# A conv-plus-experts block on one core: statistics of the first norm moved to ScalarE, sums and waits regrouped, and a new order on every engine

## What is computed

```python
x = x + conv(ln_c(x))              # ln_c: norm over the 128 channels, eps 1e-6
#   q, k, v = projections with Wq, Wkv and biases; 8 heads of 16
#   Q, K = elu(q) + 1, elu(k) + 1
#   out = causal_sum(Q, K, V) / (Q . cumsum_over_heads(K) + 1e-10)
t = x as (image, token, channel)
t = t + ffn(ln_t(t))               # ln_t: norm over the 128 channels, eps 1e-5
#   logits = t @ gate_w + router_gamma; probs = softmax; top 2 of 8 experts
#   out = sum over experts of combine * (gamma_e * (t @ expert_w[e] + expert_b[e]) + beta_e)
```

## Time and profile before

| | |
|---|---|
| median of 3 runs | 684.3 us (683.94 to 686.49) |
| the profiled execution | 687.47 us |
| its span, first to last instruction | 685.7 us |
| busy: TensorE, VectorE | 623.9 us (91%), 626.5 us (91%) |
| busy: GpSimd, ScalarE | 501.6 us (73%), 437.5 us (64%) |
| granted TensorE clock, mean over the span | 0.989 |
| DMA, mean over the span | 45 GB/s |

### The profile page before, as it was taken

One profiled execution on the slowest core, in us unless ns is written; L12 is line 12 of the kernel. 1 busy time (PEld: TensorE's weight loads), 2 busy tenths in 40 slices (PEclk: granted clock), 3 DMA queues, 4 the chain that ended last, 5 costly groups with the idle time before them and its releaser, 6 DMA issues.

```text
span 685.7 us, 37586 instructions
## 1 busy us (share of the span) xinstructions
PE 623.9 (91%) x13936; PEld 506.3 (74%) x14044; DVE 626.5 (91%) x2175; ACT 437.5 (64%) x1549; POOL 501.6 (73%) x745
## 2 busy tenths in 40 slices
PE   4769989999999999999999999999999999998875
PEld 3657777777777777777777777777777777777663
DVE  6778989999999999999999999999999999999774
ACT  1337656666667777666666667776776666667643
POOL 4747767777778888887778877878787787766631
PEclk9989999999999999999999999999999999999997
DMA  5211110111111111111111111111111121111001
GB/s 131 78 34 34 34 48 8 47 49 50 47 46 46 46 46 46 46 46 46 46 46 46 46 46 46 46 46 46 46 46 46 46 62 31 32 34 34 19 19 31
DMA packets 60234, 30.58 MB, mean 45 GB/s; under 512 B 2160, under 2 KB 60176, under 8 KB 60176
## 3 DMA queue, kind: packets, MB, share of 16 engines
q1 hardware_dynamic: 60176, 29.79, 15.5%
HBM read 20.34 MB, written 9.44 MB: 43 GB/s over the span
## 4 chain that ended last, share of the span: by engine, by line
PE 52%; DVE 24%; issue 15%; POOL 5%; DVEq 1%; ACT 1%; POOLq 0%; ACTq 0%
DVE total L824 4%; PE wide_b L1005 4%; PE num L1116 4%; PE wide_a L1212 4%; PE num L1081 3%; PE num L1099 3%; PE wide_a L1213 3%; PE wide_a L1214 3%; DVE bn L649 3%; DVE probs L696 3%; PE wide_a L1062 3%; DVE o L834 2%; PE bank_g L1037 2%; PE bank_g L975 2%; PE bank_g L1022 2%
## 5 line engine op out<-in xcount | busy, mean ns | idle before, releaser
L497 ACT ACTIVATE part<-wide_a,scale 128x128 f32<-128x128 f32 x576 | 156.3, 382 | 2.5 <-PE wide_a L1214 1.0
L373 POOL TENSOR_TENSOR two_sums<-part 128x512 f32<-128x512 f32 x72 | 92.9, 1290 | 32.0 <-ACT part L497 30.4
L1212 PE MATMUL wide_a<-e_high,x_high 128*128 128x512 f32 x216 | 97.8, 453 | 3.1 <-issue 1.1
L460 ACT ACTIVATE q_eo<-bank_g,parity 128x512 f32<-128x512 f32 x72 | 49.7, 690 | 67.5 <-PE bank_g L1037 67.5
L1214 PE MATMUL wide_a<-e_high,x_low 128*128 128x512 f32 x216 | 85.6, 396 | 0.0
L1213 PE MATMUL wide_a<-e_low,x_high 128*128 128x512 f32 x216 | 85.4, 395 | 0.0
L317 POOL TENSOR_TENSOR k_sum<-k_sum,feat 128x64 f32<-128x64 f32 x216 | 72.6, 336 | 16.9
L359 POOL TENSOR_TENSOR pack<-weight,pack 128x64 fp32r<-128x64 f32 x36 | 22.2, 616 | 77.1 <-ACT pack L505 77.1
L824 DVE SCALAR_TENSOR_TENSOR total<-wide_b,scale,total 128x128 f32<-128x128 f32 x216 | 58.8, 342 | 0.0
L824 DVE SCALAR_TENSOR_TENSOR total<-wide_a,scale,total 128x128 f32<-128x128 f32 x216 | 58.8, 342 | 0.0
L1212 PEld LDWEIGHTS wide_a<-e_high,x_high 128*128 128x128 f32 x216 | 41.6, 193 | 21.1 <-issue 17.2
(11 more groups left out here) (175 smaller groups left out, 2003.6 us busy)
## 6 DMA issues: line engine op xcount, KB each, us to landing
x<-in_x SPq DMA_DIRECT2D x36, 256.0 KB, 3.0
x_res<-in_x SPq DMA_DIRECT2D x36, 256.0 KB, 3.6
out<-o SPq DMA_DIRECT2D x36, 256.0 KB, 3.1
e_raw<-in_L_ffn_expert_w SPq DMA_DIRECT2D x1, 512.0 KB
beta_raw<-in_L_ffn_beta_w SPq DMA_DIRECT2D x1, 512.0 KB
w_raw<-in_L_conv_Wkv SPq DMA_DIRECT2D x2, 64.0 KB, 2.4
b_qkv<-in_L_conv_bkv SPq DMA_DIRECT2D x1, 128.0 KB, 5.9
w_raw<-in_L_conv_Wq SPq DMA_DIRECT2D x1, 64.0 KB, 2.6
```

Source lines behind the costliest of these rows:

```text
L373: tt(two_sums[:, g.par, two], part[:, two, 0:2], part[:, two, 2:4], ALU.add).then_inc(S[f"two_sums{p}"], 1)
L460: nc.scalar.activation(q_eo[:, g.par, :, e], bank_g[:].rearrange("p (u t) -> p u t", t=T), copy, scale=parity[:, e:e + 1]).then_inc(S[done ...
L497: last = nc.scalar.activation(part[:, u, e], w_bank[B_BANK[u]][:, 128 * e:128 * e + 128], copy, scale=scale[:, g.par, u, 4 + e:5 + e])
L1212: mm(out, x1_high[:, g.par, u], e_high[:, four], start=True, stop=False)
```

## The change

**First norm.** `statistics` and `variances` leave VectorE, with the `memset`. ScalarE now makes two passes over the four transposed images in `bank_g`: the first copies with scale and accumulates the mean, the second squares with that mean as bias and accumulates the variance. Each pass is four activations with an accumulator; the second waits for the first.

**Denominators.** `denominators_eps` moves from VectorE to ScalarE.

**Unit steps.** `add_parts` and `experts_1_to_4` handle one image instead of two, with a semaphore for each. GpSimd's four sums have 256 columns instead of two of 512. VectorE still has 16 operations a group; both halves of `two_sums` now start a sum, so that `total` has two rows and `output` transposes these.

**Coefficients.** `coef_transposed` writes `bank_o` instead of `bank_g`, and waits for `o_done` of the group before; `coefs` reads it there.

**Waits.** In the loop, the waits of `from_state`, `values` and `key_values` are put ahead of the last row of the work before them (`ahead`), and the three loads of zeros are gone. At the edges they stay.

**Order.** Every `step` is written in another order with other ages, and VectorE's and GpSimd's pipelines have 5 steps instead of 6, SP's 6 instead of 9.

**Set-up.** Five `memset`s (state, `v_pad`, `coef_t`) move from VectorE to GpSimd, and `w_t` is copied ahead of `place`.

The diff, cut to its core:

```diff
+            def means(g):
+                need(act, "squares1_done", g.i)
+                need(act, "xt_done", g.i + 1)
+                for u in range(U):
+                    last = nc.scalar.activation(squares[:, u], bank_g[:, T * u:T * u + T], copy, scale=-ROOT / CH,
+                                                accum_out=mean1[:, u:u + 1])
+                last.then_inc(S["means_done"], 1)
+
+            def variances(g):
+                need(act, "means_done", g.i + 1)
+                need(act, "ve1_done", g.i - 1)
+                for u in range(U):
+                    last = nc.scalar.activation(squares[:, u], bank_g[:, T * u:T * u + T], ACT.Square, scale=ROOT,
+                                                bias=mean1[:, u:u + 1], accum_out=ss1[:, g.par, u:u + 1])
+                last.then_inc(S["squares1_done"], 1)
...
+            def denominators_eps(g):
+                need(act, "rden_done", g.i)
+                need(act, "den_sum", g.i + 1)
+                nc.scalar.activation(den1[:], den[:], copy, bias=1e-10).then_inc(S["den_eps"], 1)
...
-            def add_parts(g, p):
-                need(pool, f"part{2 * p}", g.i + 1)
-                need(pool, f"part{2 * p + 1}", g.i + 1)
+            def add_parts(g, u):
+                need(pool, f"part{u}", g.i + 1)
                 need(pool, "out_done", g.i - 1)
-                two = slice(2 * p, 2 * p + 2)
-                tt(two_sums[:, g.par, two], part[:, two, 0:2], part[:, two, 2:4], ALU.add).then_inc(S[f"two_sums{p}"], 1)
+                tt(two_sums[:, g.par, u], part[:, u, 0:2], part[:, u, 2:4], ALU.add).then_inc(S[f"two_sums{u}"], 1)
...
+                add(0, two_sums[:, g.par, u, 0]).then_inc(done, 1)
+                add(2, two_sums[:, g.par, u, 1]).then_inc(done, 1)
+                dve.wait_ge(done, 2 * g.i + 1)
+                add(1, total[:, g.par, u, 0])
+                dve.wait_ge(done, 2 * g.i + 2)
+                add(3, total[:, g.par, u, 1]).then_inc(S[f"a_sum{u}"], 1)
...
-            def coef_transposed(g):
+            def coef_transposed(g, ahead=None):
                 need(pe, "coef_low", g.i + 1)
-                need(pe, "bn_done", g.i + 6)
+                need(pe, "o_done", g.i)
...
+                if g:
+                    experts(g, 0, 0, (lambda: values_ready(n)) if early else None)
+                g = at(4)
+                if g:
+                    values(g, early)
```

More of the change, by code:

```diff
@@ L514, in coefs @@
                     rows = slice(ROWS * u, ROWS * u + ROWS)
-                    last = nc.scalar.activation(coef_t[rows, g.par, T * u:T * u + T], bank_g[rows, 0:T], copy)
+                    last = nc.scalar.activation(coef_t[rows, g.par, T * u:T * u + T], bank_o[rows, 0:T], copy)
                 last.then_inc(S["ct_evac"], 1)
@@ L643, in expert_weights @@
                              ALU.mult, ALU.subtract))
-            def statistics(g):
-                need(dve, "stats_done", g.i)
-                need(dve, "xt_done", g.i + 1)
-                for u in range(U):
-                    last = nc.vector.bn_stats(bn[:, u], bank_g[:, T * u:T * u + T])
-                last.then_inc(S["bn_done"], 1)
-            def variances(g):
-                need(dve, "bn_done", g.i + 1)
-                need(dve, "ve1_done", g.i - 1)
-                nc.vector.memset(pause[:], 0.0)
-                for u in range(U):
-                    last = nc.vector.bn_aggr(mv1[:, g.par, u], bn[:, u])
-                last.then_inc(S["stats_done"], 1)
             def project(g, u):
@@ L1135, in x1_centred @@
                     need(pe, "lg_done", g.i)
+                    need(pe, "o_done", g.i - 1)
                 for u in range(U):
+                    if u == U - 1 and ahead:
+                        ahead()
                     out = bank_g[:, WIDE * u:WIDE * (u + 1)] if u < IN_G else bank_o[:, 0:WIDE]
@@ L1227, in output @@
                 for u in range(U):
-                    out = bank_o[:, T * u:T * u + T]
-                    mm(out, two_sums[:, g.par, u, 1], ident[:], start=False, stop=False, is_transpose=True,
-                       skip_group_check=True)
-                    last = mm(out, total[:, g.par, u], ident[:], start=False, stop=(u == U - 1), is_transpose=True,
-                              skip_group_check=True)
+                    if u == U - 1 and ahead:
+                        ahead()
+                    for k in range(2):
+                        last = mm(bank_o[:, T * u:T * u + T], total[:, g.par, u, k], ident[:], start=False,
+                                  stop=(u == U - 1 and k == 1), is_transpose=True, skip_group_check=True)
                 last.then_inc(S["out_done"], 1)
@@ L1281, in step @@
                     experts(g, 1, 1)
[L1282 removed]
+                n = at(4)
+                early = bool(n and not n.edge)
+                if g:
+                    experts(g, 0, 0, (lambda: values_ready(n)) if early else None)
                 g = at(4)
                 if g:
[L1285 removed]
+                    values(g, early)
                 g = at(5)
@@ L1295, in step @@
                 g = at(5)
+                n = at(3)
+                early = bool(n and not n.edge)
                 if g:
-                    experts(g, 3, 0)
+                    experts(g, 3, 0, (lambda: key_values_ready(n)) if early else None)
+                g = at(3)
+                if g:
+                    key_values(g, early)
+                g = at(5)
+                if g:
+                    experts(g, 2, 0)
+                g = at(1)
+                if g:
+                    project(g, 2)
+                    project(g, 3)
+                g = at(3)
+                if g:
+                    if first(g):
+                        router()
+                    q_transposed(g)
+                g = at(1)
+                if g:
+                    project(g, 1)
+                    project(g, 0)
             steps(pe, step, 6)
```

429 lines of the change are left out of this document (207 added, 222 removed).

## The result

The changed kernel takes 784.15 us (median of four runs, 782.29 to 799.96), the kernel before 684.74 in the same session. The ratio is 1.144, 95% interval 1.140 to 1.147: slower by a seventh, where 645.7 us and a gain were forecast. The run of 799.96 us was a slow one, over 1.5% above the fastest, and is not in the ratio. The profiled execution has a span of 782.5 us against 685.7.

What follows compares the result with a forecast made beforehand. VectorE was taken as the bound, TensorE half a microsecond behind. A turn of 16.45 instead of 17.43 us gave loop 24.5, turns ahead 5.9, filling and set-up 1.2 + 3, end 4: 38.6 off 684.3, so 645.7 us; range 628 to 664.

Steps and rivals of the forecast that it cites:

- GpSimd has room: GpSimd's four unit sums replace two longer ones: 0.4 us more a turn, absorbed because others rarely wait for it.
- TensorE* does the same matmuls: TensorE's loop: matmuls unchanged, three loads of zeros gone; its turn becomes 16.1 to 16.9 us, 16.5 chosen.
- ScalarE's passes: First norm's statistics on ScalarE: eight accumulating activations, 0.25 us each in the first pass, 0.34 in the second.
- the rival that ended slower: ScalarE's two passes do not overlap accumulator readings, so ScalarE sets the pace at 18.0 us a turn: 696 us; chance 0.07.
- The wait for the unit sum: At VectorE's first expert sum: VectorE waits 0.2 us a turn for ScalarE's and GpSimd's work.
- `coef_transposed` waiting for the output: On TensorE, `coef_transposed` now waits for `o_done`, VectorE's output; costed at nothing.
- The ring through the keys' copy: ScalarE's `pexp` ahead of the keys' copy, which frees `bank_g`: eats the gain, 17.4 us a turn, 680 to 684; chance 0.05.
- The 1.31: VectorE loses `bn_stats`, `memset`, `bn_aggr` and the epsilon: 1.31 us less a turn, from 17.43 to 16.1.
- The wait of `rden` for the epsilon: On VectorE, `rden` waits for the epsilon queued on ScalarE: 0.4 us a turn.
- they cost nothing there: VectorE keeps 16 expert operations in steps of two, so the unit sums add nothing on it.
- TensorE's zeros: Removing the three loads of zeros from TensorE's loop saves 0.4 us a turn, between 0 and about 0.8.
- The set-up: Ahead of the first projection: moved `memset`s let it start at about 11 instead of 14.11, 3 us saved.

Runs made afterwards that it cites:

- e1: The changed kernel with 64 loads of zeros put once into TensorE's set-up: 727.27 us, ratio 1.0625 to the kernel before.
- e4: e1 with GpSimd's queries-times-keys product waiting for VectorE's ranks of the others and the low part of x behind it: 678.52 us, ratio 0.990.
- e12: e4 with GpSimd's long product waiting for VectorE's equal instead of the ranks behind it: 672.2 us, ratio 0.980.
- e9: e4 with VectorE's router chain filled as in the kernel before and ScalarE's router exponential moved behind values and keys: 677.17 us.
- e7: e4 with ScalarE's router exponential moved from ahead of the values and keys to behind them: 677.37 us.
- e5: e4 with the three loads of zeros back in every turn of TensorE's loop, each behind its own waits: 681.48 us.
- e8: e4 with the first norm's statistics on VectorE again and none on ScalarE: 700.89 us, ratio 1.023.
- e2: The kernel before with 195 loads of zeros put once into TensorE's set-up: 789.43 us, ratio 1.151.
- e3: The kernel before with 100 loads of zeros put once into TensorE's set-up: 693.24 us, ratio 1.011.
- e11: The kernel before with 165 loads of zeros put once into TensorE's set-up: 708.17 us, ratio 1.034.

## Why the prediction was wrong, step by step

**The frame.** That GpSimd has room and that SP costs nothing were answers to one question only, who waits for whom by semaphores; the text ahead of the prediction says that the engines meet only there. Both causes of the loss lie outside that: GpSimd held VectorE up without a semaphore (62 rows of e1), and TensorE stood still for its own code. The step that failed first is GpSimd's, "0.4 more a turn, and has room": its price was right (a unit sum takes 745 ns, 0.74 was taken), but nobody asked what its moved operations stand beside.

```profile
L374 POOL TENSOR_TENSOR two_sums<-part 128x256 f32<-128x256 f32 x144 | 105.8, 745 | 54.4 <-ACT part L527 53.5
```

The orders of both engines were there to be read: `x_low` and `qk` had moved to where VectorE runs the router's chain. 1.6 us a group, 49 us (e1 to e4), and 6 more to e12. The second failure is "*TensorE* does the same matmuls". It does, and its loop is even a record shorter; but the set-up and the edge turns ahead of it changed length, and its code came to lie on seven marks: 57 us (after to e1), the lower clock behind the stalls included. No term, no rival and no chance stood for it. The trace of before did show the transfers that end at 176 us and begin again at 600, but the prediction didn't read them.

**What held.** ScalarE's passes, in after, are 0.26 (forecast 0.25) and 0.36 (0.34) apart:

```profile
418.12 0.28 ACT L436 ACTIVATE squares<-bank_g 128x128 f32<-128x128 f32 x1 [0.26 <-PE bank_g L977]
...
418.38 0.27 ACT L436 ACTIVATE squares<-bank_g 128x128 f32<-128x128 f32 x1
...
419.29 0.37 ACT L444 ACTIVATE squares<-bank_g,mean 128x128 f32<-128x128 f32 x1
...
419.65 0.36 ACT L444 ACTIVATE squares<-bank_g,mean 128x128 f32<-128x128 f32 x1
```

So ScalarE doesn't set the pace; the rival that ended slower named the wrong engine and the wrong mechanism. The wait for the unit sum is 0.2 as forecast (the distance at the residual add, 0.79 against 0.62). `coef_transposed` waiting for the output is real and cost nothing, as said (e9). The ring through the keys' copy is real and cost nothing (e7).

**What was mis-sized**, seen once both causes are out of the way (distances of VectorE's starts a group, us, mean of 20 groups of before, e4 and e1):

| rows of VectorE | before | e4 | e1 |
|---|---|---|---|
| statistics, epsilon | 1.31 | 0 | 0 |
| output | 0.81 | 0.60 | 0.60 |
| residual add | 0.62 | 0.79 | 0.77 |
| 16 expert rows | 4.21 | 4.37 | 4.42 |
| key-value masks | 0.40 | 0.54 | 0.54 |
| first two router rows | 0.37 | 0.65 | 0.65 |
| two hot rows | 0.45 | 0.78 | 0.49 |
| logits of the others, equal, ranks | 0.53 | 0.52 | 2.25 |
| hot sum, weight | 0.34 | 0.58 | 0.58 |
| all rows | 17.46 | 17.19 | 18.78 |

The 1.31 and the 0.2 of the output went as forecast. The wait of `rden` for the epsilon, forecast 0.4, is 0.1 in e4; it was in after, where ScalarE was late, 16.5 us in 28. What was left out are the rows that the new order made longer: the expert rows, "they cost nothing there", 0.16; the key-value masks, the router's first two rows, the hot sum and weight together 0.7; and `hot`, held by GpSimd, 0.3. So the turn is 17.19 and, without most of the hold, 16.96 (e12), not 16.45. TensorE's zeros were put at 0.4 and are 0.15 (e5). The set-up was put at 3 us; the first projection comes only 1.0 earlier than in the earlier trace rows, at

```profile
13.10 0.67 PE L1007 MATMUL wide_b<-w_high,x_high 128*128 128x384 f32 x1
```

because TensorE waited 3.78 us for `w_t` and 1.24 for `w_low` ahead of it, and not for the second `x`.

**The sum.** From 784.2: 57 us for the code, 49 and 6 for the contention, leads to 672.2. Of the 26.5 from there to the forecast, the starts of the outputs place 24. In the kernel before the first starts at 79.38 us, the 7th, the 32nd and the last as in the earlier trace rows; in e12 these four start at 78.00, 185.29, 609.18 and 667.72. So the 25 groups of the loop gain 11.8 us and not 24.5, the six ahead of them 3.6 and not 5.9, set-up and filling 1.4 and not 4.2, and the last four groups, which were to gain 4, lose 2.2. The first two go with VectorE's longer turn; what makes the end slower is not shown. The mechanism that the prediction counted on, work from a full engine to one with room, is there and is worth 22 us (e8). It was outweighed by two costs that no row of a wait announces.

## What to carry to other kernels

Before a loop of many matmuls is changed, or anything ahead of it, count its TensorE instructions and see over how many 16 KB blocks it lies; look whether the transfers of instructions stop once the loop runs. Some dozens of instructions more or less in the set-up decided it here (64 loads, 784.2 to 727.3 us), and it should be ruled out ahead of any story about waits. When GpSimd's order moves, lay both engines' rows side by side: a long GpSimd operation belongs beside VectorE work that reads PSUM or one tile, not beside a chain of short operations on two.

## What the runs showed of the hardware

- TensorE's loop of 1616 or 1617 records (two groups) stayed in place in every turn on seven blocks of 256 records, and on eight it was fetched again in 3 to 12 turns of twelve. A refetched turn costs 3.3 to 5.9 us at the branch, and with what follows 5.7 us in the changed kernel (57 / 10) and 8.0 in the kernel before (e2 against e3, 96 / 12).
- Around the end of such a stall TensorE's granted clock fell to half (1.2 GHz), for 6.8 us in ten of the twelve refetched turns of e2 and in all three of e11; in after it fell in seven of the ten.
- With the last block entered only 12 records ahead of the branch, three turns of twelve were fetched again, with 39 to 44 records ten to twelve.
- A VectorE operation of 0.19 us with two inputs in SBUF lasted up to 1.26 us in e1 beside a GpSimd operation of 1.27 us, until 0.05 us after its end.
- 100 loads of zeros in the set-up took 1.91 us, 19 ns apart (e3).
